# Self-attention stage of a fused two-layer block: where the row sums and the projections stand among the slots

## Chip, cores, metric

One core of one Trainium2 chip. The metric is the device time of one launch in microseconds; the median over runs counts. A profiled execution of the same kernel gives the trace.

## What is computed

The program is a stack of four blocks on x of 16 x 256 x 128 (batches, tokens, channels): an attention with a cross part, a gated feed-forward net, a pre-norm self-attention followed by a cross-attention (each with its own feed-forward net), and a routed expert layer. The change touches only the self-attention ("a1") of the third block. Cut to what matters, for each of the 16 batches and 16 heads of width 32:

```python
xn = _ln(x, lnx_g, lnx_b); yn = _ln(y, lny_g, lny_b)          # x is itself a LayerNorm of a LayerNorm
q = einsum('bsc,hcd->bhsd', xn, wq); k, v likewise from yn    # y is x here
a = softmax(einsum('bhsd,bhtd->bhst', q, k) * D ** -0.5)
mask = arange(t)[None, :] > arange(s)[:, None]                # causal: kept AFTER the softmax
o = einsum('bhst,bhtd->bhsd', a * mask, v)
x_out = x + o @ li1_w + li1_b
```

The softmax sums run over all 256 keys, the values only over the masked part, so sums and values are two different sets of products.

## The kernel before, in words

Every engine runs one program in the order in which it was written; semaphores tie the five programs together. The order inside this stage is written by hand in **slots**. `SelfAttention` has U = 8 slots to a batch; slot s belongs to unit s, a pair of heads. All four engines have a function for a slot (`tensor_slot` L1550, `vector_slot` L1621, `scalar_slot` L1686, `gpsimd_slot` L1731), and dictionaries (`SLOT` L1326, `VECTOR` L1327, `EARLY` L1328 for the last two batches) say at which slot, counted from 8n, each piece of batch n stands. Below, "slot 0" to "slot 7" is a slot's number modulo 8. `run` (L1757) emits slots 15 to 129; slots up to 14 are emitted between the products of the feed-forward stage before it (`l0_ffn`, L834, 16 slots to a step), the rest of the tail by `mha_ffn`. The parts of one slot:

- **Block** (`tensor_block`, L1474): 12 scores products and 12 products for the row maxima of a unit nine slots ahead, each on 32 rows of the array by 128 columns (L1499, L1504), then four products that subtract the maxima (L1511). The maxima go to PSUM banks 2 and 3, a single set: the next block waits until VectorE has reduced them (L1583). The scores go to banks 0 and 1, also a single set before batch 15: the next block waits for ScalarE's exp (L1668).
- **Sums** (`tensor_sums`, L1515) and **values** (`tensor_values`, L1532) of a group of four heads: products on 128 rows by 32 columns of the array. Sums of groups 0 to 3 stand at slots 2, 4, 6 and 8, values at 3, 5, 7 and 9, so that every slot has one of the two.
- **Projections** (`tensor_projection`, L1431), products on the whole array of 128 x 128: q0 at slot 0, k0 at 1, q1 at 2, k1 at 3, v0 at 4, v1 at 5, and at slot 6 z (two transposes), o (16 products, from slot 22 on) and nm (two transposes of the maxima). They share banks 5 and 7 through a ring of two. A q or k goes out through ScalarE (high half, L1652) and then VectorE (low half, L1593, one slot later); z goes out by four ScalarE activations (L1647). The third product of q0 (L1454) waits for `z_low`, which GpSimd writes (L1723) behind its select of slot 7 (L1705).
- **VectorE**, per slot: the maximum, then low halves of the projections of the slot before, then the pieces of `VECTOR` in its order: rden (L1611) and the first normalise (part 1, L187 on `b_zi`) in slot 6; scaled (L1619) in slot 0; stats of part 2 in slot 2; stats of part 0 (L150 to L159) in slot 4; second normalise (part 3, L187 on `b_z`) in slot 5; output in slot 7. Part 1 waits for GpSimd's reciprocal root (`gpsimd_rstd`, L161, of the kind "twice": six small operations, L172 to L181), which starts from the stats of part 0. Part 3 releases z.
- **ScalarE**, per slot: exp, the copy of the sums (L1684, slot 9), the copy of the values (L1676, slots 6 and 10), then the projections of the slot.

The piece of code that sets the order on TensorE:

```python
def tensor_slot(self, s):
    self.tensor_block(s)
    for g, n in self.parts(s, {0: 2, 1: 4, 2: 6, 3: 8}): self.tensor_sums(n, g)
    for g, n in self.parts(s, {0: 3, 1: 5, 2: 7, 3: 9}): self.tensor_values(n, g)
    for use in self.parts(s, self.SLOT): self.tensor_projection(use)
```

Of the kernel before, what the change touches and what calls it, by code (L numbers as in the profile page):

```python
# [241 lines left out]
def l0_attention(pr, mem, ffn, meanwhile):  # L242
# [56 lines left out]
    for i in range(3):  # L299
        nc.vector.memset(V[i][:, :, :, D:D + 1], 1.0)  # L300
        for a in range(2):
# [18 lines left out]

    SLOT = {"z": -28, "q0": -20, "q1": -16, "v": -14, "k": -15, "qk0": -24, "kc": -13, "ck": -23, "cv": -13,
            "qk1": -22, "nm": -3, "e0": 12, "e1": 13, "e2": 13, "e3": 18, "e4": 20}
# [3 lines left out]
    def batches(n, u, slots):  # L326

        pairs = [(part, *divmod(U * n + u - slot, U)) for part, slot in slots.items()]
        return [(part, batch) for part, batch, rest in pairs if rest == 0 and 0 <= batch < B]

    def projections(n, u):
        return batches(n, u, SLOT)

# [442 lines left out]
    for slot in (tensor_slot, vector_slot, scalar_slot, gpsimd_slot):  # L776
        for s in range(U * FIRST, tail):
            slot(s)
    sync_program()
    return Tail(tail, last, tensor_slot, vector_slot, scalar_slot, gpsimd_slot, exp_done, U * B, ys_ready, 3 * B,  # L780
                av_done, NV * B, x_done)

# [531 lines left out]
class SelfAttention:  # L1314
# [8 lines left out]

    U, G, D = 8, 4, 32

    SLOT = {"z": -18, "q0": -16, "k0": -15, "q1": -14, "k1": -13, "v0": -12, "v1": -11, "o": 22, "nm": -2}  # L1326
    VECTOR = {"rden": 14, "scaled": 16, "output": 23, 0: -28, 1: -26, 2: -22, 3: -19}  # L1327
    EARLY = {"o": 15, "rden": 9, "scaled": 12, "output": 16}  # L1328
    FIRST_MAX, FIRST, LAST = -9, -28, 8 * (B - 1) + 16
    tail_vector, tail = 8 * B + 1, 8 * B + 2  # L1330
# [3 lines left out]
    def __init__(self, pr, mem, tag, w):  # L1334
# [30 lines left out]
        for s in range(self.FIRST, self.LAST + 1):  # L1365
            for use in self.parts(s, self.SLOT):
                self.ring.add(use, "v" if use[0][0] in "qk" else "a")
# [181 lines left out]

    def tensor_slot(self, s):  # L1550
        self.tensor_block(s)
        for g, n in self.parts(s, {0: 2, 1: 4, 2: 6, 3: 8}):
            self.tensor_sums(n, g)
        for g, n in self.parts(s, {0: 3, 1: 5, 2: 7, 3: 9}):
            self.tensor_values(n, g)
        for use in self.parts(s, self.SLOT):
            self.tensor_projection(use)
# [63 lines left out]
    def vector_slot(self, s):  # L1621
        nx, m = divmod(s - self.FIRST_MAX, self.U)
        if 0 <= nx < B:
            self.vector_max(nx, m)
        for use in self.parts(s - 1, self.SLOT):
            if use[0][0] in "qk":
                self.vector_low(use)
        for part, n in self.parts(s, self.VECTOR):
            if part == "rden":
# [56 lines left out]
    def scalar_slot(self, s):  # L1686
# [5 lines left out]
        for half, n in self.parts(s, {0: 6, 1: 10}):  # L1692
            self.scalar_values(n, half)
        for use in self.parts(s, self.SLOT):
            self.scalar_projection(use)
# [76 lines left out]
class CrossAttention:  # L1772
# [10 lines left out]
    SLOT = {"z": -11, "k": -8, "q0": -7, "q1": -6, "v": -4, "nm": -1, "o": 14}  # L1783
    SCORES, VALUES, MAXIMA = {0: 0, 1: 2}, {0: 3, 1: 5}, -4
# [952 lines left out]
```

## Time and profile before

| | us |
|---|---|
| median of 3 runs | 1507.75 |
| the three runs | 1508.36, 1507.75, 1500.03 |
| profiled execution, its own time | 1501.43 |
| its span in the trace | 1499.7 |
| TensorE busy in the span | 1351.0 (90%) |
| VectorE / ScalarE / GpSimd busy | 977.7 / 845.7 / 649.5 |
| this stage alone (slot 15 to slot 129) | about 660 to 1015 in the span |

Mean granted clock of TensorE over the span: 0.967. A row of the timeline reads: start in us, duration in us, engine, line, operation, output <- inputs, shapes, count, and in brackets how long the engine was idle before it and what released it.

### The profile page before, as it was taken

Reading aid. Unit: us, or ns where it says so; the run is one execution under the profiler, and the core shown is the slowest. Engines: PE = TensorE matmul, PEld = TensorE weight load, DVE = VectorE, ACT = ScalarE, POOL = GpSimd, SP = SyncE. Lnnn points to the kernel's source line nnn. Section 1 sums busy time; section 2 is a strip of 40 time slices with the busy share of each in tenths; the row PEclk is TensorE's granted clock in tenths of the full one; section 3 lists DMA queues with packets and bytes.
Section 4 is the critical chain, followed back from the end, with each engine's and each line's share of the span. In section 5 each row is a group of like instructions: output and inputs, shape, how many; then the busy total and the mean of one; then the engine's idle time right before and its main releaser. Section 6 shows DMA issues by size and latency. Waiting matters only on the chain.

```text
span 1499.7 us, 42738 instructions
## 1 busy us (share of the span) xinstructions
PE 1351.0 (90%) x17848; PEld 856.9 (57%) x17848; DVE 977.7 (65%) x2238; ACT 845.7 (56%) x1309; POOL 649.5 (43%) x1118
## 2 busy tenths in 40 slices
PE   5899999997899998899999999997989999998695
PEld 2455555554344444455666666664766777677484
DVE  4777777775454544577788787745667887675232
ACT  2577777775465555657666666653456666432231
POOL 3355545543200001335666566343337775354155
PEclk9999999998999999999999999998999999998798
DMA  6000000000600000000000000012001111032351
GB/s 214 3 3 2 3 2 3 3 3 2 161 1 1 1 1 0 1 2 17 30 17 31 30 17 31 22 39 57 1 16 45 56 48 45 29 99 73 122 158 43
DMA packets 54514, 53.76 MB, mean 36 GB/s; under 512 B 9273, under 2 KB 48574, under 8 KB 54067
## 3 DMA queue, kind: packets, MB, share of 16 engines
q1 hardware_dynamic: 50482, 44.24, 9.7%
q0 software_dynamic: 2816, 6.11, 1.2%
q8 instruction: 142, 2.33, 0.7%
q10 hardware_dynamic: 1024, 0.69, 0.2%
q14 instruction: 50, 0.40, 0.1%
HBM read 20.34 MB, written 14.49 MB: 23 GB/s over the span
## 4 chain that ended last, share of the span: by engine, by line
PE 65%; DVE 12%; ACT 6%; issue 5%; POOL 5%; DMA 3%; SPq 3%; POOLq 0%; DVEq 0%; ACTq 0%
PE psum L1499 6%; PE psum L911 4%; PE psum L913 3%; PE psum L912 3%; PE psum L1182 3%; PE psum L1527 3%; DVE a_nm L580 3%; PE psum L1148 3%; PE psum L2496 2%; PE psum L2512 2%; PE psum L1976 2%; SPq L772 2%; DMA a_QT<-a_nmT 2%; DVE b_nm L1583 2%; PE psum L1985 2%
## 5 line engine op out<-in xcount | busy, mean ns | idle before, releaser
L1583 DVE TENSOR_REDUCE b_nm<-psum 128x4 f16<-128x1024 f32 x128 | 157.5, 1230 | 70.0 <-PE psum L1504 69.0
L697 ACT ACTIVATE a_prob<-psum 128x768 f32<-128x768 f32 (+1 forms) x160 | 136.1, 853 | 62.5 <-PE psum L460 60.6
L580 DVE TENSOR_REDUCE a_nm<-psum 128x4 f16<-128x1024 f32 (+1 forms) x96 | 117.4, 1223 | 50.2 <-PE psum L487 35.8
L749 POOL TENSOR_SCALAR_AFFINE_SELECT a_prob<-a_prob 128x512 f32<-128x512 f32 x128 | 81.7, 639 | 129.5 <-ACT a_prob L697 129.3
L170 POOL TENSOR_TENSOR f_ln_rstd<-f_ln_tmp,pow_half 128x4 f32<-128x4 f32 x24 | 25.3, 1056 | 204.6 <-DVE f_ln_tmp L159 204.6
L1040 ACT ACTIVATE xo_sb<-psum,f_w_h_s 128x512 f32<-128x512 f32 x64 | 44.0, 688 | 87.0 <-PE psum L913 87.0
L1499 PE MATMUL psum<-b_QTh,b_KTh 32*128 32x256 f16 x512 | 71.2, 272 | 11.7 <-DVE b_nm L1583 8.5
L1504 PE MATMUL psum<-b_KTh,b_QTh 32*128 32x256 f16 x512 | 70.7, 273 | 1.5 <-DVE b_nm L1583 1.5
L1499 PE MATMUL psum<-b_QTh,b_KTl 32*128 32x256 f16 x512 | 70.2, 268 | 0.0
L1499 PE MATMUL psum<-b_QTl,b_KTh 32*128 32x256 f16 x512 | 70.2, 267 | 0.0
L1504 PE MATMUL psum<-b_KTl,b_QTh 32*128 32x256 f16 x512 | 69.5, 268 | 0.0
L1504 PE MATMUL psum<-b_KTh,b_QTl 32*128 32x256 f16 x512 | 69.5, 268 | 0.0
L1705 POOL TENSOR_SCALAR_AFFINE_SELECT b_late<-f_hT1l 128x256 f32<-128x256 f32 x64 | 28.2, 463 | 88.7 <-ACT f_hT1l L1668 88.7
L2606 POOL DMA_INDIRECT out_dram<-m_ys,m_number x40 | 39.7, 991 | 55.2 <-DVE m_ys L2547 45.1
L980 DVE TENSOR_TENSOR f_hlastl<-xo_sb,f_hlasth 128x512 f16<-128x512 f32 x32 | 22.2, 692 | 53.0 <-ACT f_hlasth L1041 53.0
L980 DVE TENSOR_TENSOR f_hT1l<-xo_sb,f_hT1h 128x512 f16<-128x512 f32 x32 | 22.5, 702 | 51.6 <-ACT f_hT1h L1041 51.6
L911 PE MATMUL psum<-f_hT0h,f_h_wh 128*128 128x512 f16 x128 | 50.1, 392 | 5.9 <-DVE f_hT0l L974 5.9
L1499 PEld LDWEIGHTS psum<-b_QTh,b_KTh 32*128 32x128 f16 x512 | 25.4, 92 | 45.3 <-issue 27.8
L913 PE MATMUL psum<-f_hT0h,f_h_wl 128*128 128x512 f16 x128 | 50.0, 391 | 0.0
L912 PE MATMUL psum<-f_hT0l,f_h_wh 128*128 128x512 f16 x128 | 49.8, 389 | 0.0
L1511 PE MATMUL psum<-b_nmT,b_group_row 32*128 32x256 f16 x512 | 49.1, 268 | 0.0
L1668 ACT ACTIVATE f_hT0h<-psum 128x1024 f32<-128x1024 f32 x32 | 32.7, 1023 | 28.2 <-PE psum L1511 28.2
(448 smaller groups left out, 4637.8 us busy)
## 6 DMA issues: line engine op xcount, KB each, us to landing
f_h_wh<-b_rden SPq DMA_DIRECT2D x64, 128.0 KB, 2.1
f_h_wh<-c_rden SPq DMA_DIRECT2D x64, 128.0 KB, 2.1
expert_in<-empty SPq DMA_DIRECT2D x8, 662.5 KB, 11.0
m_xt<-expert_in SPq DMA_DIRECT2D x8, 662.5 KB
m_w<-in_L_ffn_w_dram SPq DMA_DIRECT2D x16, 256.0 KB
x_sb<-in_x_dram SPq DMA_DIRECT2D x8, 256.0 KB, 4.6
f_w_h_w<-in_L_ffn_h_w_dram SPq DMA_DIRECT2D x2, 1024.0 KB, 7.5
out_dram<-m_send SPq DMA_DIRECT2D x8, 256.0 KB, 2.5
```

The costliest lines, as they stand in the source:

```text
L580: nc.vector.tensor_reduce(out, psum[:, 2:4, :].rearrange("p i (a b) -> p i a b", a=groups), X, ALU.max, negate=True).then_inc(max_done, 1)
L697: nc.scalar.activation(prob[unit % 5][:, :, 0:width], psum[:, first:first + 2, 0:width], ACT.Exp, scale=SCALE).then_inc(exp_done, 1)
L749: nc.gpsimd.affine_select(out=diagonal, in_=diagonal, compare_op=ALU.is_ge, fill=0.0, base=0, pattern=[[0, 4], [1, P]], channel_multiplier ...
L911: nc.tensor.matmul(bank, wh[:, k, m * P:m * P + P], xh[:, k, :], start=(k == 0), stop=False)
L912: nc.tensor.matmul(bank, wh[:, k, m * P:m * P + P], xl[:, k, :], start=False, stop=False)
L913: inst = nc.tensor.matmul(bank, wl[:, k, m * P:m * P + P], xh[:, k, :], start=False, stop=(k == K4 - 1))
L1148: nc.tensor.matmul(psum[:, u % 3, :], li2[:, slot * P:slot * P + P], zT[n % 2][:, :], start=True, stop=True).then_inc(full, 1)
L1182: inst = nc.tensor.matmul(bank[:, to], hT[n % 2][:, k, to], li3[:, k, :], start=(t == 0 and k == 0), stop=True, skip_group_check=True)
L1499: t.matmul(psum[:, first_bank + i, to], key[r, g, own], q[r, g, :], start=(k + first + second == 0), stop=False, skip_group_check=True)
L1504: inst = t.matmul(psum[:, 2 + i, to], q[r, g, own], key[r, g, :], start=(k + first + second == 0), stop=(first == 1), skip_group_check=True)
L1511: inst = t.matmul(psum[:, first_bank + i, k * T:k * T + T], self.group_row[r, g, :], self.nmT[n % 2][r, :], start=False, stop=True, skip_g ...
L1583: v.tensor_reduce(self.nm[:, :, :].rearrange("p t (j r) -> p j t r", r=32)[:, 2 * e:2 * e + 2, :, g], self.pr.psum[:, 2:4, :].rearrange("p ...
```

## The change

Four edits, all of order; no instruction is added or removed.

1. `SLOT`: k0 moves from slot 1 to slot 0 (beside q0), k1 from 3 to 2 (beside q1), v1 from 5 to 4 (beside v0). Their exits on ScalarE, and the low halves on VectorE, move with them.
2. Sums move one slot later, to 3, 5, 7 and 9, right ahead of the values of the same group.
3. `VECTOR`: part 1 moves from -26 (slot 6, behind rden) to -27 (slot 5, ahead of part 3).
4. The slots of the values get a name.

```diff
-    SLOT = {"z": -18, "q0": -16, "k0": -15, "q1": -14, "k1": -13, "v0": -12, "v1": -11, "o": 22, "nm": -2}
-    VECTOR = {"rden": 14, "scaled": 16, "output": 23, 0: -28, 1: -26, 2: -22, 3: -19}
+    SLOT = {"z": -18, "q0": -16, "k0": -16, "q1": -14, "k1": -14, "v0": -12, "v1": -12, "o": 22, "nm": -2}
+    VALUES = {0: 3, 1: 5, 2: 7, 3: 9}
+    VECTOR = {"rden": 14, "scaled": 16, "output": 23, 0: -28, 1: -27, 2: -22, 3: -19}
...
     def tensor_slot(self, s):
         self.tensor_block(s)
-        for g, n in self.parts(s, {0: 2, 1: 4, 2: 6, 3: 8}):
+        for g, n in self.parts(s, self.VALUES):
             self.tensor_sums(n, g)
-        for g, n in self.parts(s, {0: 3, 1: 5, 2: 7, 3: 9}):
             self.tensor_values(n, g)
         for use in self.parts(s, self.SLOT):
             self.tensor_projection(use)
```

## Rows read from the trace of the kernel before

**Rows 1.** The page, first part: busy time of each engine.

```profile
PE 1351.0 (90%) x17848; PEld 856.9 (57%) x17848; DVE 977.7 (65%) x2238; ACT 845.7 (56%) x1309; POOL 649.5 (43%) x1118
```

**Rows 2.** Timeline of VectorE: maxima of slots 54, 55, 57, 58, 62, 110, one low half.

```profile
809.66 1.23 DVE L1583 TENSOR_REDUCE b_nm<-psum 128x4 f16<-128x1024 f32 x1 [0.79 <-PE psum L1504]
...
814.36 1.23 DVE L1583 TENSOR_REDUCE b_nm<-psum 128x4 f16<-128x1024 f32 x1 [1.39 <-PE psum L1504]
...
819.48 1.23 DVE L1583 TENSOR_REDUCE b_nm<-psum 128x4 f16<-128x1024 f32 x1 [0.41 <-PE psum L1504]
...
820.62 0.68 DVE L1593 TENSOR_TENSOR b_QTl<-psum,b_QTh 128x512 f16<-128x512 f32 x1
...
822.01 1.23 DVE L1583 TENSOR_REDUCE b_nm<-psum 128x4 f16<-128x1024 f32 x1 [0.71 <-PE psum L1504]
...
832.54 1.23 DVE L1583 TENSOR_REDUCE b_nm<-psum 128x4 f16<-128x1024 f32 x1 [0.79 <-PE psum L1504]
...
969.78 1.23 DVE L1583 TENSOR_REDUCE b_nm<-psum 128x4 f16<-128x1024 f32 x1 [1.29 <-PE psum L1504]
```

**Rows 3.** Timeline of TensorE, first instruction of the parts of slots 54 to 58.

```profile
809.75 0.41 PE L1527 MATMUL psum<-f_hT0h,b_group_col 128*32 128x256 f32 x2
...
810.75 0.44 PE L1439 MATMUL psum<-ident,b_z 128*128 128x128 f32 x2
...
813.25 0.28 PE L1464 MATMUL psum<-ident,b_nm 128*128 128x128 f16 x2 [0.27 <-ACT b_zTyh L1647]
813.47 0.28 PE L1499 MATMUL psum<-b_QTh,b_KTh 32*128 32x256 f16 x2
...
814.44 0.30 PE L1543 MATMUL psum<-f_hT0h,b_V 128*32 128x128 f32 x2
...
815.73 0.28 PE L1499 MATMUL psum<-b_QTh,b_KTh 32*128 32x256 f16 x2 [0.43 <-DVE b_nm L1583]
...
818.05 0.28 PE L1454 MATMUL psum<-b_zTxl,b_wqh 128*128 128x256 f16 x1
...
819.56 0.30 PE L1543 MATMUL psum<-f_hT1h,b_V 128*32 128x128 f32 x2
...
820.36 0.28 PE L1450 MATMUL psum<-b_zTyh,b_wkh 128*128 128x256 f16 x1
...
821.12 0.28 PE L1499 MATMUL psum<-b_QTh,b_KTh 32*128 32x256 f16 x2
```

**Rows 4.** Timeline of TensorE in the feed-forward stage: a block directly ahead of a whole-array product.

```profile
623.36 0.27 PE L1504 MATMUL psum<-b_KTl,b_QTh 32*128 32x256 f16 x2
623.47 0.27 PE L1504 MATMUL psum<-b_KTh,b_QTl 32*128 32x256 f16 x2
623.67 0.39 PE L911 MATMUL psum<-f_hT0h,f_h_wh 128*128 128x512 f16 x1
```

**Rows 5.** Timeline of GpSimd: select of slot 55, low of z, first and last step of a reciprocal root.

```profile
815.65 1.07 POOL L1705 TENSOR_SCALAR_AFFINE_SELECT b_late<-f_hT1l 128x256 f32<-128x256 f32 x2 [3.92 <-ACT f_hT1l L1668]
...
817.33 0.66 POOL L1723 TENSOR_TENSOR b_zTyl<-b_zTy,b_zTyh 128x256 f16<-128x256 f32 x1
...
830.07 0.69 POOL L172 TENSOR_TENSOR b_lni_tmp<-b_lni_tmp,pow_one 128x2 f32<-128x2 f32 x1 [0.72 <-DVE b_lni_tmp L159]
...
832.98 0.20 POOL L181 TENSOR_TENSOR b_lni_rstd<-b_lni_rstd,b_lni_tmp 128x2 f32<-128x2 f32 x1
```

**Rows 6.** Timeline of ScalarE in slot 54: the first activation of z.

```profile
811.26 0.57 ACT L1647 ACTIVATE b_zTx<-psum,b_w_bx,b_w_gx 128x256 f32<-128x256 f32 x1
```

**Rows 7.** Timeline of VectorE in the feed-forward stage, around part 1 of batches 1 and 2.

```profile
602.34 0.60 DVE L187 TENSOR_SCALAR b_z<-u_sb,b_lnx_mv,b_lnx_rstd 128x128 f32<-128x128 f32 x2
...
618.30 0.75 DVE L969 SCALAR_TENSOR_TENSOR xo_sb<-psum,f_w_w_s,xo_sb 128x512 f32<-128x512 f32 x1 [0.60 <-PE psum L904]
...
620.90 0.60 DVE L187 TENSOR_SCALAR b_zi<-x_sb,b_lni_mv,b_lni_rstd 128x128 f32<-128x128 f32 x2 [1.25 <-POOL b_lni_rstd L181]
```

**Rows 8.** Timeline of GpSimd there: last step of the reciprocal root of batch 1.

```profile
603.66 0.19 POOL L181 TENSOR_TENSOR b_lni_rstd<-b_lni_rstd,b_lni_tmp 128x2 f32<-128x2 f32 x1
```

## The prediction

> **What bounds the kernel now.** I read the page's busy shares first, then the timelines of TensorE, VectorE, GpSimd and ScalarE over one batch of the stage. TensorE is busy 90% of the span [rows 1], but that is no proof that each slot is bound by it, so I went slot by slot. The maximum of slot 54 starts at 809.66, that of slot 62 at 832.54, that of slot 110 at 969.78 [rows 2]: 22.88 for one batch, and (969.78 - 809.66) / 7 = 22.87 for the seven up to there. The pattern repeats exactly from the batch in which o first stands (slot 22) to slot 110, eleven times. Within it:
> - Slot 6 lasts 814.36 - 809.66 = 4.70 [rows 2]. The nm transposes waited 0.27 for the last activation of z on ScalarE [rows 3], so the end of slot 6 is ScalarE's: exp, copy of the values, four activations of z. TensorE's own work there is hidden.
> - Slot 7 lasts 815.73 - 813.47 = 2.26; the next block waited 0.43 for the maximum [rows 3]. This is VectorE's floor for any slot: its maximum begins 814.36 - 813.47 = 0.89 behind the block and the next block 1.37 behind that [rows 2, 3].
> - Slots 0 to 5 are TensorE's. Slots 7 and 0 together are 819.48 - 814.36 = 5.12, slot 1 is 822.01 - 819.48 = 2.53, slots 2 to 5 are 832.54 - 822.01 = 10.53 [rows 2].
>
> **What a turn of the array costs.** In a block successive steps stand 0.11 apart, but from its last step to a whole-array product it is 623.67 - 623.47 = 0.20 [rows 4]: 0.09 for the change of shape. A k projection is six steps of 0.107, 0.64, yet the next block comes 821.12 - 820.36 = 0.76 after its start [rows 3]: 0.12. So a turn is about 0.09 to 0.13. Parts with the turn behind them: block 814.44 - 813.47 = 0.97, sums 810.75 - 809.75 = 1.00, values 820.36 - 819.56 = 0.80, q or k (v likewise, three products of twice the columns) 0.76 [rows 3]. Sums and values use the array in the same shape, so between them I take no turn: sums 0.87. Bounds: 0 and 0.13 for it.
>
> [...]
>
> **The change, one batch.**
> - Slots 2 to 5. Even ones become block + two projections, 0.97 + 0.64 + 0.76 = 2.37; odd ones block + sums + values, 0.97 + 0.87 + 0.80 = 2.64. Four slots are 10.02 instead of 10.53: -0.5. With a turn of 0.13 between sums and values it is -0.25; I take -0.45. Even slots stay above the floor of 2.26 by 0.11, and VectorE's two low halves now follow each other: the low begins 820.62 - 819.48 = 1.14 after the maximum and takes 0.68, of which some 0.6 is its own time [rows 2], so both end 2.4 after the maximum, before the next one, due after 2.64.
> - Slot 1: 2.64 to 2.67 instead of 2.53: +0.13. It loses k0 and gets the last sums.
> - Slots 7 and 0. The sums of group 2 leave slot 6, where they were hidden, for slot 7, whose 2.26 was VectorE's: it becomes about 2.66. Slot 0 then cannot use that delay: q0's third product needs the low half of z. GpSimd starts the select of slot 7 at 815.65 and ends the second low at 817.33 + 0.66 = 817.99 [rows 5], and the product went at 818.05, 4.58 behind block 7's start [rows 3]. That chain (exp of slot 7, select, two lows) hangs on block 7 and not on what TensorE does after it, so it stays 4.58. TensorE would now be there at 2.66 + 0.97 + 0.22 = 3.85, and waits 0.73. Behind it come four q0 steps, 0.43, and k0 with its turn, 0.76: 4.58 + 1.19 = 5.77 instead of 5.12: +0.65. What queues behind the waiting product: k0, block 1, and so the next maximum; nothing else fills TensorE.
> - Slot 6. Taking the sums out gives nothing, since ScalarE's chain sets its end. And part 1 is now in slot 5, in VectorE's queue ahead of part 3 and of the maximum of slot 6. Its root takes GpSimd 832.98 + 0.20 - 830.07 = 3.11 [rows 5] and was ready at 833.18, 0.64 after the maximum of slot 6 began [rows 2]. The stats start 0.60 earlier (k1's low no longer stands ahead of them), but slots 4 and 5 are 0.21 shorter, so the root comes 0.64 - 0.60 + 0.21 = 0.25 after the moment when that maximum is due. Then a hop of about 0.1, part 1 and part 3 (two normalise operations each, 0.60 a part in rows 7, some 0.45 when another follows at once): the maximum starts 1.4 late and z is released only then. Before, z went to TensorE 810.75 - 809.66 = 1.09 and to ScalarE 811.26 - 809.66 = 1.60 after the maximum [rows 2, 3, 6]; now TensorE gets it at about 1.44 and ScalarE at 1.95. So z, which was followed by everything else on ScalarE, is 0.35 later: +0.35. The late maximum itself is covered by slot 6's length, and so is rden behind it, barely (it ends about when block 7 starts; the next maximum is 0.89 later). Bounds: 0, if the root comes in time, and +1.4, if nothing covers it.
>
> Batch: -0.45 + 0.13 + 0.65 + 0.35 = +0.68. Eleven of them: +7.5.
>
> **The rest of the stage.** The two batches of slots 6 to 21 have no o; there exp of slot 7 waits behind z and the same two waits bite: +0.7 each, 1.4. At the end no projections are left: slots 110 and 118 lose the sums' 1.00 each; slots 111, 113, 115, 117 and 119 go from 2.26 to 2.66, +2.0; slots 120 to 127 lose a turn or two per pair, four times 0.25. Together -1.0.
>
> In the feed-forward stage ahead, slots are long, but VectorE's queue also holds that stage's own work. Part 1 of batch 2 waited 1.25 there, at 620.90 [rows 7]. One slot earlier it stands ahead of part 3 and of the gated product of 618.30 [rows 7], which would then start at 620.9 + 0.45 + 0.60 = 621.95, 3.65 late; z's four activations stand in ScalarE's queue ahead of the next GELU, so TensorE's next layer is up to 3.6 late too. For batch 1 the root ended at 603.66 + 0.19 [rows 8] while part 3 ran at 602.34 [rows 7]: z would be released 2.1 late, of which TensorE had about 0.9 idle to spare: 1.2. The two are 4.8 at most; some is absorbed where TensorE later waited for VectorE anyway. I take +4.0, bounds 0 and +6.
>
> Other edits: the order in the ring of banks is the same (q0, k0, q1, ...), so each part gets the bank that it had; the exits on ScalarE move with their slot and stay ahead of the next exp; the SyncE queue is untouched, rden and its four transfers keep their slots; naming the slots is nothing.
>
> **Sum.** +7.5 + 1.4 - 1.0 + 4.0 = +11.9. On the profiled execution's own 1501.43 that is 1513.3. Two of the three runs shown stand some 7 above it; on the median, 1507.75, it is 1519.7, and I give 1519.5.
>
> **Rivals.**
> - *Only the junctions and slot 7 matter.* Part 1 costs nothing (GpSimd's root is in time, or the feed-forward stage swallows it). Then a batch is +0.34 (0.65 + 0.13 - 0.45), thirteen of them 4.4, less 1.0: 1507.75 + 3.4 = 1511. For it: much of what part 1 delays is idle time; against it: 0.25 late by the rows, in strict order. 15%.
> - *Faster: both waits on GpSimd are hidden.* The place is q0's third product. If the low half of z landed by 3.85 behind block 7 instead of 4.58 (a shorter select and shorter lows, if the 1.07 of rows 5 was a collision with VectorE), slots 7 and 0 would be 5.04, -0.08, and with part 1 free the batch 0.13 - 0.45 - 0.08 = -0.40. Thirteen: -5.2, less 1.0: 1507.75 - 6.2 = 1501.5. It decides from 0.4 us gained on that chain. Against it: the exp and the select alone take 815.65 + 1.07 - 813.47 = 3.25 [rows 3, 5], and nothing in the change shortens them. 10%.
> - *The stall spreads.* Part 1's wait pushes the maximum, rden, its transfers and the late selects, and slot 6 grows by 1.0 to 1.4 rather than 0.35: +0.7 to +1.0 a batch more, 9 to 13 in all: 1530. For it: rden is covered by nothing to spare. 20%.
>
> **How the numbers follow.** Forecast 55%, the others 15, 10 and 20. About 1%, 15 us, is what a measurement of this kernel can tell from no change. The forecast's own range is 1512 to 1526, of which its top, 12 points, lies over +1%; the spreading stall lies over it nearly whole: slower 0.31. Of the fast rival 3 points are beyond -1%; the rest is within. The range for eight in ten reaches down to the fast rival's middle and up to the start of the spreading stall: 1503 to 1528.
>
> **What would show it.** In the profile after: no gap longer than 0.03 between sums and values, even slots of 2.37 and odd ones of 2.65 between maxima; in slot 0 a wait of some 0.7 at L1454 for GpSimd's low; part 1 on VectorE idle some 1.8 for the root (2.64 from maximum to maximum, less 1.14, plus 0.35), and the maximum of slot 6 late by 1.4; slots 6 of 5.05; a batch of 23.55. Wrong it would be if a batch came under 22.9, if L1454 didn't wait, or if the block of slot 7 waited for a maximum.

## The result, and the profile after

| | us |
|---|---|
| changed kernel, median of 4 runs | 1525.43 (1522.93 to 1529.46) |
| kernel before, 4 runs beside them | 1506.87 (1500.03 to 1508.36) |
| ratio, 95% interval | 1.0134 (1.0107 to 1.0162) |
| profiled execution after: own time, span | 1524.46, 1522.7 |
| profiled execution before: span | 1499.7 |

The kernel became 1.3% slower, 18.6 us by the medians and 23.0 by the two spans. The forecast was 1519.5, within 1503 to 1528. Most of its signs and places were right, the end of the stage was not, and the sum (+11.9) was too small. The mean granted clock is 0.954 (0.967 before).

The page's first part, of the kernel after, against [rows 1]: busy times hardly moved, the span grew. What came is waiting.

```profile
PE 1346.2 (88%) x17848; PEld 870.0 (57%) x17848; DVE 979.8 (64%) x2238; ACT 841.3 (55%) x1309; POOL 648.6 (43%) x1118
```

VectorE's timeline after, slots 52 to 57 (slots 4, 5, 6, 7, 0 and 1 of a batch), against [rows 2]:

```profile
811.55 1.23 DVE L1584 TENSOR_REDUCE b_nm<-psum 128x4 f16<-128x1024 f32 x1 [0.21 <-PE psum L1506]
...
813.93 1.23 DVE L1584 TENSOR_REDUCE b_nm<-psum 128x4 f16<-128x1024 f32 x1 [0.27 <-PE psum L1506]
816.85 0.69 DVE L187 TENSOR_SCALAR b_zi<-x_sb,b_lni_mv,b_lni_rstd 128x128 f32<-128x128 f32 x2 [1.69 <-POOL b_lni_rstd L181]
817.46 0.59 DVE L187 TENSOR_SCALAR b_z<-u_sb,b_lnx_mv,b_lnx_rstd 128x128 f32<-128x128 f32 x2
817.97 1.22 DVE L1584 TENSOR_REDUCE b_nm<-psum 128x4 f16<-128x1024 f32 x1
...
821.73 1.23 DVE L1584 TENSOR_REDUCE b_nm<-psum 128x4 f16<-128x1024 f32 x1 [0.89 <-PE psum L1506]
...
824.37 1.23 DVE L1584 TENSOR_REDUCE b_nm<-psum 128x4 f16<-128x1024 f32 x1 [0.54 <-PE psum L1506]
...
827.50 1.23 DVE L1584 TENSOR_REDUCE b_nm<-psum 128x4 f16<-128x1024 f32 x1 [0.37 <-PE psum L1506]
```

The third line is the first new wait: part 1 idles 1.69 for the root (forecast 1.8), part 3 and the maximum stand behind it, and that maximum starts at 817.97 where 813.93 + 2.64 = 816.57 was due: 1.40 late, as forecast. The next three rows give slots 6, 7 and 0 from maximum to maximum: 3.76, 2.64, 3.13.

TensorE's timeline after, slots 54 to 57, against [rows 3]:

```profile
818.19 0.41 PE L1441 MATMUL psum<-ident,b_z 128*128 128x128 f32 x2 [1.47 <-DVE b_z L187]
...
820.63 0.28 PE L1466 MATMUL psum<-ident,b_nm 128*128 128x128 f16 x2 [0.24 <-ACT b_zTyh L1648]
820.85 0.28 PE L1501 MATMUL psum<-b_QTh,b_KTh 32*128 32x256 f16 x2
...
821.82 0.41 PE L1529 MATMUL psum<-f_hT0h,b_group_col 128*32 128x256 f32 x2
...
822.28 0.39 PE L1529 MATMUL psum<-f_hT0h,b_group_col 128*32 128x256 f32 x2
...
822.50 0.39 PE L1529 MATMUL psum<-f_hT0h,b_group_col 128*32 128x256 f32 x2
...
822.71 0.28 PE L1545 MATMUL psum<-f_hT0h,b_V 128*32 128x128 f32 x2
...
823.48 0.28 PE L1501 MATMUL psum<-b_QTh,b_KTh 32*128 32x256 f16 x2
...
825.41 0.28 PE L1456 MATMUL psum<-b_zTxl,b_wqh 128*128 128x256 f16 x1 [0.56 <-POOL b_zTyl L1724]
...
826.61 0.28 PE L1501 MATMUL psum<-b_QTh,b_KTh 32*128 32x256 f16 x2
```

Three readings. From the last sums step to the values it is 822.71 - 822.50 = 0.21, the pace within the sums themselves (822.50 - 822.28 = 0.22): between two parts of one shape there is no turn. The product of L1456 waits 0.56 for the low half of z, the second new wait; it goes 825.41 - 820.85 = 4.56 behind block 7 (forecast 4.58, before 4.58), and block 1 goes 5.76 behind it (forecast 5.77). The idle of 1.47 ahead of z is not all loss: ScalarE's chain sets the end of slot 6, and before the change the sums filled part of that time.

GpSimd's timeline after, the chain of that low half, against [rows 5]: the select is released by the exp of slot 7 and again takes 1.07, both lows follow.

```profile
823.03 1.07 POOL L1706 TENSOR_SCALAR_AFFINE_SELECT b_late<-f_hT1l 128x256 f32<-128x256 f32 x2 [4.36 <-ACT f_hT1l L1669]
...
824.70 0.67 POOL L1724 TENSOR_TENSOR b_zTyl<-b_zTy,b_zTyh 128x256 f16<-128x256 f32 x1
```

The waits of TensorE after, from 690 to 940 us (engine, line, waited for: us in total, times, longest), show both in every batch:

```profile
PE psum L1441 <- DVE b_z L187: 16.2, 11, 1.5
PE psum L1456 <- POOL b_zTyl L1724: 5.1, 9, 0.6
PE psum L1466 <- ACT b_zTyh L1648: 2.4, 10, 0.2
```

Before, the same view had none of the first two:

```profile
PE psum L1499 <- DVE b_nm L1583: 4.3, 10, 0.4
PE psum L1464 <- ACT b_zTyh L1647: 2.7, 10, 0.3
```

VectorE's timeline after, in the last steps of the feed-forward stage ahead, against [rows 7]. Part 1 of batch 1 waits 1.54, that of batch 2 3.19 (before: none and 1.25), and here part 3 and the gated product are behind it.

```profile
599.16 0.60 DVE L187 TENSOR_SCALAR b_zi<-x_sb,b_lni_mv,b_lni_rstd 128x128 f32<-128x128 f32 x2 [1.54 <-POOL b_lni_rstd L181]
...
617.24 0.60 DVE L187 TENSOR_SCALAR b_zi<-x_sb,b_lni_mv,b_lni_rstd 128x128 f32<-128x128 f32 x2 [3.19 <-POOL b_lni_rstd L181]
617.76 0.60 DVE L187 TENSOR_SCALAR b_z<-u_sb,b_lnx_mv,b_lnx_rstd 128x128 f32<-128x128 f32 x2
618.27 0.75 DVE L969 SCALAR_TENSOR_TENSOR xo_sb<-psum,f_w_w_s,xo_sb 128x512 f32<-128x512 f32 x1
```

The end of the stage after, VectorE's timeline: here something came that no step had foreseen. The scaled products of batches 12 and 13 (batches are counted from 0) wait 1.93 and 5.41 for the broadcast of rden. The first and third rows are the maxima of slots 110 and 111.

```profile
981.35 1.23 DVE L1584 TENSOR_REDUCE b_nm<-psum 128x4 f16<-128x1024 f32 x1 [1.40 <-PE psum L1506]
982.49 1.74 DVE L1612 RECIPROCAL b_rden<-b_sums 128x256 f32<-128x256 f32 x1
984.42 1.23 DVE L1584 TENSOR_REDUCE b_nm<-psum 128x4 f16<-128x1024 f32 x1 [0.19 <-PE psum L1506]
...
990.22 1.23 DVE L1620 TENSOR_TENSOR f_h_wl<-f_h_wh 128x1024 f32<-128x1024 f32 x1 [1.93 <-DMA f_h_wh<-b_rden]
...
1004.55 1.74 DVE L1612 RECIPROCAL b_rden<-b_sums 128x256 f32<-128x256 f32 x1
...
1012.44 1.22 DVE L1620 TENSOR_TENSOR f_h_wl<-f_h_wl,f_h_wh 128x1024 f32<-128x1024 f32 x1 [5.41 <-DMA f_h_wh<-b_rden]
```

TensorE's next sums wait for the rden of batch 14, which stands behind the second of these waits in VectorE's queue:

```profile
1015.48 0.41 PE L1529 MATMUL psum<-f_hT0h,b_group_col 128*32 128x256 f32 x2 [2.65 <-DVE b_rden L1612]
```

Before, batch 12 had no wait on VectorE, and batch 13 had 2.44:

```profile
990.83 1.74 DVE L1611 RECIPROCAL b_rden<-b_sums 128x256 f32<-128x256 f32 x1
...
996.61 1.23 DVE L1619 TENSOR_TENSOR f_h_wl<-f_h_wl,f_h_wh 128x1024 f32<-128x1024 f32 x1 [2.44 <-DMA f_h_wh<-b_rden]
```

Where the 23.0 us of the two spans went, by stretches between the same instructions. The first stretch ends at the last GELU ahead of the last step of the feed-forward stage (603.02 before, 598.22 after); the next ones end at the maxima of slots 7, 23, 95 and 111, and at the first product of the next feed-forward stage. The forecast's -1.0 for slots 110 to 127 is split here by place: the 1.00 of slot 110 belongs to the stretch up to slot 111, which leaves 0.0 for the rest.

| stretch | before | after | difference | forecast |
|---|---|---|---|---|
| up to the last feed-forward step | 603.0 | 598.2 | -4.8 | 0 |
| from there to slot 7 | 74.6 | 82.1 | +7.5 | +4.0 |
| slots 7 to 23 (two batches, no o) | 45.2 | 47.0 | +1.8 | +1.4 |
| slots 23 to 95 (nine batches) | 205.9 | 212.5 | +6.6 | +6.1 |
| slots 95 to 111 (two batches) | 45.1 | 44.7 | -0.5 | +0.4 |
| slot 111 to the next stage | 47.0 | 53.3 | +6.3 | 0.0 |
| the rest of the program | 478.9 | 485.0 | +6.1 | 0 |

A full batch takes 212.47 / 9 = 23.61. Its eight slots after, from maximum to maximum, slot 6 first: 3.77, 2.63, 3.13, 2.63, 2.40, 2.63, 2.38, 4.03 (sum 23.60); before: 4.69, 2.26, 2.86, 2.53, 2.74, 2.53, 2.73, 2.53 (22.87). Slot 5's 4.03 holds the late maximum: without its 1.40 it is 2.63, and slot 6 is 5.17.

### The profile page after: what moved, and what is told of

It is laid out like the page before. It is cut to its first block, busy times and chain, and to the rows that moved or that the text cites. A ratio compares the mean times of both kernels' runs of the same rounds, so it can differ in the third digit from the quotient of the medians.

```text
span 1522.7 us, 42738 instructions
## 1 busy us (share of the span) xinstructions
PE 1346.2 (88%) x17848; PEld 870.0 (57%) x17848; DVE 979.8 (64%) x2238; ACT 841.3 (55%) x1309; POOL 648.6 (43%) x1118
## 4 chain that ended last, share of the span: by engine, by line
PE 55%; DVE 14%; POOL 10%; issue 8%; ACT 5%; DMA 4%; SPq 3%; POOLq 0%; DVEq 0%; ACTq 0%
PE psum L1501 4%; PE psum L1182 3%; PE psum L911 3%; PE psum L913 3%; PE psum L912 3%; DVE a_nm L580 3%; PE psum L1148 3%; PE psum L1529 2%; PE psum L2497 2%; PE psum L2513 2%; SPq L772 2%; POOL b_late L1706 2%; DMA a_QT<-a_nmT 2%; PE psum L1977 2%; DVE b_nm L1584 2%
## 5 line engine op out<-in xcount | busy, mean ns | idle before, releaser
L1669 ACT ACTIVATE f_hT1h<-psum 128x1024 f32<-128x1024 f32 x32 | 32.8, 1024 | 48.4 <-PE psum L1513 48.4
L911 PE MATMUL psum<-f_hT0h,f_h_wh 128*128 128x512 f16 x128 | 49.4, 386 | 6.6 <-DVE f_hT0l L974 6.6
```

The costliest lines, as they stand in the source:

```text
L911: nc.tensor.matmul(bank, wh[:, k, m * P:m * P + P], xh[:, k, :], start=(k == 0), stop=False)
L1669: a.activation(self.prob[unit % 4][:, :, :], self.pr.psum[:, first:first + 2, :], ACT.Exp, scale=self.SCALE).then_inc(self.exp_done, 1)
```

## The experiments

In all of them "batch" is the mean of slots 23 to 95 of the profiled execution, and "end" the stretch from slot 111 to the next feed-forward stage. A ratio is to the kernel before on the same chip. Kernels that ran only once have no interval; they are read by their stretches, which are steadier than whole times.

**The changed kernel again**, unedited, to see what is steady between executions.

> The changed kernel once more, to see which of its 18.6 us (1525.4 against 1506.9) come back in the same places. Theory A (waits by their place in strict queues): a steady batch of slots 22 to 94 lasts 23.60 again, the stall of VectorE for the four transfers of rden at slot 112 and the TensorE idle at slot 123 come again, ratio to before 1.013. Theory B (the part of the loss that lies behind the stage, some 6 us, is only the clock's history of one execution): batches as in A, but that part is gone or has another size.

Measured: 1523.73 (4 runs), ratio 1.0122 (1.0081 to 1.0164). Batch 23.60; up to slot 7 81.3 where the first profile had 82.1; end 50.6 where it had 53.3. The waits of VectorE at slot 112 (1.77) and of TensorE for the rden of batch 14 (1.81) came again, and the rest of the program took 485.4, as in the first profile: theory B is not borne out. So the batch repeats within 0.01, the end to 2.6 us.

**Part 1 back to its slot.**

```diff
-    VECTOR = {..., 0: -28, 1: -27, 2: -22, 3: -19}
+    VECTOR = {..., 0: -28, 1: -26, 2: -22, 3: -19}
```

> The changed kernel with part 1 of VectorE back in slot 6 behind rden. Theory A: slot 6 loses 0.35 and the maximum of slot 6 is on time, batch 23.25; the last step of the feed-forward stage ahead comes 3 to 4.5 us earlier; 8 to 10 us below the changed kernel, ratio to before about 1.007. Theory C (the two waits hide one another: with z earlier, q0 just waits longer for the low half of z): batch still over 23.5, and under 5 us in all.

Measured: 1510.08 (10 runs), ratio 1.0039 (1.0014 to 1.0064): 13.7 us less than the changed kernel beside it, where 8 to 10 had been expected. Up to slot 7 it takes 74.1, as before the change, 7.2 less than again; batch 23.14, 0.46 less; slots 7 to 23 1.0 less. The waits of TensorE, 690 to 940:

```profile
PE psum L1466 <- ACT b_zTyh L1648: 12.8, 10, 1.3
PE psum L1456 <- POOL b_zTyl L1724: 6.4, 11, 0.7
```

The wait for z is gone, and most of that idle time has moved to the nm transposes (1.3 for ScalarE): TensorE is no fuller in slot 6, the slot ends earlier all the same. So part 1's place is the largest single cost of the change, and of what it cost beyond the forecast (13.7 against 8.6) two thirds lie ahead of slot 7 (7.2 against 4.0).

**The low half of z one slot earlier on GpSimd**, ahead of the select of slot 7.

```diff
-        for part, n in self.parts(s, {"low": -17, ...}):
+        for part, n in self.parts(s, {"low": -18, ...}):
```

> The changed kernel with the low half of z on GpSimd one slot earlier (slot 6, ahead of the select of slot 7 instead of behind it); part 1 stays in slot 5. Theory A: the third product of q0 waits for nothing, slots 7 and 0 lose 0.7, batch 22.9, 9 to 10 us below the changed kernel, ratio to before about 1.006. Theory C: the late z of slot 6 is what counts, GpSimd's select of slot 7 now comes late instead and holds the values of slot 1 or the exp, batch over 23.4.

Measured: 1515.70 (7 runs), ratio 1.0082 (1.0048 to 1.0115), 8.0 us less than again (9 to 10 expected). Batch 22.96: four of the nine take 22.87, which is 0.73 less than again, and five take 23.01 to 23.08. In the same stretch VectorE waited five times, 1.9 us in all, for the transfers of rden. Slots 7 to 23 gain nothing. The waits of TensorE, 690 to 940: the line of L1456 is gone and nothing took its place.

```profile
PE psum L1441 <- DVE b_z L187: 16.1, 11, 1.5
```

**Both edits together.** Does one wait hide the other, or do they add?

> Both: part 1 back in slot 6 and the low half of z in slot 6 on GpSimd. Theory A: the two add up, batch 22.6, about 0.3 below the kernel before; the feed-forward stage as before; the tail still costs some 5 us, so ratio to before 0.997 to 1.002. Theory C: not below 23.2. If the grouping of sums and values cost TensorE time by itself, the odd slots would stay above 2.64.

Measured: 1502.28 (10 runs), ratio 0.9974 (0.9951 to 0.9997). Less than again by 21.5, against 13.7 + 8.0 = 21.7 for the two alone: they add, and the idea that one hides behind the other falls. Batch 22.47, which is -0.40 to before; five of the nine take 22.39, -0.48. This is the regrouping alone (the fast rival had -0.40 for it). Nine batches are 3.6 shorter than before, but the end is 50.1, 3.1 longer, and takes most of that back; with the smaller gains of the other stretches the stage as a whole is 4.4 shorter.

**Where should the sums of group 2 stand?** In both, with them left in slot 6, where they are hidden:

```diff
-        for g, n in self.parts(s, self.VALUES):
+        for g, n in self.parts(s, {0: 3, 1: 5, 2: 6, 3: 9}):
             self.tensor_sums(n, g)
+        for g, n in self.parts(s, self.VALUES):
             self.tensor_values(n, g)
```

> Both moves of the run before, and the sums of group 2 stay in slot 6, where the kernel before had them (groups 0, 1 and 3 stand with their values in slots 3, 5 and 9). Theory A: slot 6 is ScalarE's, so the sums cost nothing there, slot 7 goes back to VectorE's floor of 2.26, and the distance from rden to scaled grows by nothing less than before: batch 22.0, some 0.9 below the kernel before; ratio 0.989 to 0.992. Theory D (the sums in slot 6 were not hidden; the gain of 'both' needs the pairs everywhere): batch not below 22.4.

Measured: 1496.50 (10 runs), ratio 0.9935 (0.9913 to 0.9957), so 0.65% faster than the kernel before (0.989 to 0.992 had been expected). Batch 22.03, end 46.6. VectorE's timeline of it, slots 7, 0 and 1:

```profile
831.86 1.23 DVE L1585 TENSOR_REDUCE b_nm<-psum 128x4 f16<-128x1024 f32 x1 [1.39 <-PE psum L1506]
...
834.12 1.23 DVE L1585 TENSOR_REDUCE b_nm<-psum 128x4 f16<-128x1024 f32 x1 [0.16 <-PE psum L1506]
...
836.73 1.22 DVE L1585 TENSOR_REDUCE b_nm<-psum 128x4 f16<-128x1024 f32 x1
```

Slot 7 is at VectorE's floor again, 834.12 - 831.86 = 2.26, and slot 0 is 2.61: with the low half early, the 0.37 saved in slot 7 are no longer waited away in slot 0.

**The same move of the sums in the changed kernel itself**, both waits left in.

> The changed kernel with the sums of group 2 back in slot 6 and nothing else. Theory A: slot 7 falls from 2.63 to 2.26, but the low half of z hangs on block 7 and q0's third product waits that much longer, so slots 7 and 0 stay 5.77 together and a batch 23.60. Theory G (the move of the sums out of slot 6 is what costs): batch 23.2.

Measured (one run): 1526.21. Batch 23.60, unchanged to the hundredth: slot 7 shrinks to 2.26 and slot 0 grows to 3.50. So the product that waits for the low half is tied to block 7, as the forecast had it, and not to what TensorE does in between. But the end is 47.0, as long as before the change (again: 50.6): the longer end comes with the sums of group 2 in slot 7. All fourteen profiles of this document agree: six have these sums in slot 7 and rden at its old slot, with ends of 49.4 to 53.3; the other eight have ends of 46.6 to 47.4.

**One half of the regrouping at a time, in the kernel before.** First the sums alone, with their values:

```diff
-        for g, n in self.parts(s, {0: 2, 1: 4, 2: 6, 3: 8}): self.tensor_sums(n, g)
+        for g, n in self.parts(s, {0: 3, 1: 5, 2: 7, 3: 9}): self.tensor_sums(n, g)
```

> The kernel before with the sums alone moved beside the values; the projections stay one to a slot. Theory A: odd slots become block, sums, values, projection, 0.97 + 0.87 + 0.80 + 0.76 = 3.4, while even slots cannot go under VectorE's floor of 2.26: batch 24.3 to 24.6, 20 us or more above the kernel before, although TensorE has fewer turns. Theory E (turns are what counts): batch below 22.9.

Measured (one run): 1531.07, batch 24.51, +1.64. Its waits of TensorE, 700 to 960:

```profile
PE psum L1464 <- ACT b_zTyh L1647: 12.7, 10, 1.3
PE psum L1499 <- DVE b_nm L1583: 9.7, 21, 0.5
PE psum L1454 <- POOL b_zTyl L1723: 6.3, 11, 0.7
```

Then the projections alone, two to an even slot:

```diff
-    SLOT = {"z": -18, "q0": -16, "k0": -15, "q1": -14, "k1": -13, "v0": -12, "v1": -11, ...}
+    SLOT = {"z": -18, "q0": -16, "k0": -16, "q1": -14, "k1": -14, "v0": -12, "v1": -12, ...}
```

> The kernel before with the projections alone paired in even slots. Theory A: even slots 0.97 + 1.00 + 0.64 + 0.76 = 3.4, odd ones at the floor of 2.26: batch 23.6 to 23.9, some 12 us above the kernel before. Theory E: about as before, 22.9.

Measured (one run): 1518.44, batch 24.04, +1.16. Its waits of TensorE, 700 to 960:

```profile
PE psum L1499 <- DVE b_nm L1583: 17.9, 42, 0.4
```

Each half alone takes turns of the array away and is slower. A slot that loses a part falls only to what VectorE needs, while its neighbour pays the part in full. With the projections alone, the odd slots take 2.26 to 2.34 and TensorE waits there (17.9 us in 42 blocks, about four in each batch), and the even ones 3.31 to 3.52. With the sums alone, slots 2 and 4 take 2.61 and not 2.26: VectorE works through them without a pause, on the maximum, a low half and the stats of a part, so the floor of these slots is higher than that of slot 7. Only the two halves together leave the slots even, 2.38 and 2.63. The batch with the sums alone lies in the expected range, the one with the projections alone above it (24.04 where 23.6 to 23.9 was expected).

**Part 1 one slot earlier, in the kernel before.**

```diff
-    VECTOR = {..., 0: -28, 1: -26, 2: -22, 3: -19}
+    VECTOR = {..., 0: -28, 1: -27, 2: -22, 3: -19}
```

> The kernel before with part 1 of VectorE alone in slot 5. Theory A: z late by VectorE's wait for the root: 7 to 8 us lost before slot 7 of the first batch as in the changed kernel, and 0.4 to 0.7 a batch, batch 23.3 to 23.6; 12 to 16 us above the kernel before. Theory C (the wait costs only where slots 4 and 5 are already shortened): batch 22.9.

Measured (one run): 1533.06, batch 24.27, +1.40, far more than in the changed kernel. Its waits of VectorE, 700 to 960:

```profile
DVE b_zi L187 <- POOL b_lni_rstd L181: 21.3, 11, 1.9
DVE f_h_wl L1619 <- DMA f_h_wh<-b_rden: 7.5, 7, 1.9
```

The expectation missed. In the kernel before, the low half of k1 stands ahead of the stats of part 0, so the root is later: part 1 starts 0.64 after the moment when the maximum of slot 6 was due, and 0.28 after it in the changed kernel. z goes to TensorE 2.28 after that moment, and slot 6, counted from it, takes 5.82 where it took 4.69 (in the changed kernel 1.62 and 5.17). Six of the nine batches take 24.01, +1.14, which is this and nothing else. The other three take 24.15 to 25.45 and make up the remaining 0.26 of the mean; that they are longer by VectorE's waits for rden's transfers fits the view above, but was not tried. The regrouping, then, made part 1's new place cheaper, not dearer. Ahead of slot 7 the damage is about the same as in the changed kernel (82.4 against 74.6).

**The low half early, in the kernel before.**

> The kernel before with the low half of z alone moved ahead of the select of slot 7 on GpSimd. Theory A: with q0 behind the sums it hardly waited, so only the 0.1 of slot 0 goes: batch 22.75 to 22.87. Theory H (GpSimd's order was a cost of its own in the kernel before): batch under 22.5.

Measured (one run): 1505.19 beside 1505.99; batch 22.77, 0.1 less. Before the change there was nothing there to win: the edit matters only once TensorE arrives early.

**Rden one slot earlier**, at slot 13 and behind part 3, first in the kernel with both edits:

```diff
-    VECTOR = {"rden": 14, "scaled": 16, "output": 23, 0: -28, 1: -26, 2: -22, 3: -19}
+    VECTOR = {"scaled": 16, "output": 23, 0: -28, 1: -26, 2: -22, 3: -19, "rden": 13}
```

> The run 'both' with rden one slot earlier, in slot 5 behind part 3 instead of slot 6, so that its four transfers have 1.6 us more before scaled asks for them. Theory A (the end of the stage loses its time because the shorter slots leave the transfers of rden no room: VectorE waits for them at slot 112, and at slots 118 to 123 this holds rden of batch 14, so TensorE idles for some 3 us and its granted clock falls): those waits go, from slot 111 to the next stage 47 us instead of 50.1, granted clock 1.00 there, batches 22.40 throughout instead of 22.39 to 22.70. Theory F (the end is slow for the longer odd slots alone): 111 to the next stage stays near 50.

Measured: 1496.93 (4 runs), ratio 0.9939 (0.9919 to 0.9958). Batch 22.40, end 46.6, that is 3.5 less than in both. At the end of the stage VectorE has no wait for batch 12 and 0.80 for batch 13, where both has 2.06 and 5.28. (The edit moves the rden of batches 0 to 13; the last two keep theirs, by `EARLY`.)

```profile
986.84 1.23 DVE L1620 TENSOR_TENSOR f_h_wl<-f_h_wl,f_h_wh 128x1024 f32<-128x1024 f32 x1 [0.80 <-DMA f_h_wh<-b_rden]
```

**The same in the kernel called best above.**

> The run 'best' with rden one slot earlier as well. Theory A: a batch stays 22.03, since slots 7 to 1 are bound by VectorE's maxima, scaled and low halves there, and the few late transfers go: from slot 111 to the next stage 46 or less, 1 to 2 us below 'best' at most; ratio 0.990 to 0.994. If rden in slot 5 made the maximum of slot 6 late enough to hold nm, the batch would be above 22.3.

Measured: 1497.58 (8 runs), ratio 0.9944 (0.9924 to 0.9964), batch 22.03, end 47.0. Nothing more is won, against an expected end of 46 or less: the two cures for the end don't add, as each already removes the same late transfers. The three fastest kernels can't be told apart; each beats both the kernel before and the changed one.

## Why the prediction was right, and where it was not

**Right by its own steps.** Slots 2 to 5: forecast -0.45, measured 2.40 + 2.63 + 2.38 + 2.63 = 10.04 against 10.53, -0.49. Slot 1: +0.13, measured +0.10. Slots 7 and 0: +0.65, measured 2.63 + 3.13 = 5.76 against 5.12, +0.64, by the mechanism named (the wait itself was 0.56 and not 0.73, since TensorE got there at 4.00 and not 3.85, but the product goes by the low half of z, at 4.56); with the low half early it vanished, and after_g2 showed that it hangs on block 7. No turn between sums and values; even slots 2.38 to 2.40 (forecast 2.37), odd ones 2.63 (2.65). The batch: 23.60 against 23.55. Nine batches and the two without o cost 8.4 (forecast 7.5). The Trainium skill (TensorE: Matmul & The Clock Gate, Single matmul latency) puts the time for results to drain from the array at roughly 175 ns; as an estimate from that page, taking it as the price of each of four turns saved, slots 2 to 5 would have won 4 x 0.175 = 0.70. The measurement is -0.49, nearer to the 0.09 to 0.13 a turn that the rows of the kernel before gave.

**Slot 6, the term mis-sized.** "+0.35" was +0.48. The root came 0.17 after the moment when the maximum was due (it ended at 816.54 + 0.20 = 816.74 on GpSimd, against 816.57), a little sooner than my 0.25, but the two normalise parts took 0.61 and 0.59 where I had taken "some 0.45 when another follows at once". So z went to TensorE 818.19 - 816.57 = 1.62 after that moment instead of 1.44.

**The feed-forward stage ahead, the term mis-sized.** "I take +4.0" was +7.5 up to slot 7 in the first profile and +6.7 in the second; with part 1 back it was -0.5. I had added up two waits at the places where they stand (1.2 and 3.6, in full 4.8) and let some be absorbed. Nothing was absorbed: by the two profiles, 1.7 and 1.4 were lost ahead of the last step, where z of batch 1 was late (for the 1.2), and 4.3 in both within that step, from its first SiLU to its last sum on VectorE (for the 3.6). Another 1.5 and 1.0 came between the step and slot 7, for which I had no term. Part 1 altogether: forecast 0.35 x 13 + 4.0 = 8.6, measured 13.7 by the medians. That is where most of the gap between +11.9 and the +18.6 of the medians lies.

**The end of the stage, the step that failed.** "At the end no projections are left: ... Together -1.0." There I had counted TensorE's parts only. Those came out: slot 110 took 4.07 before (969.78 to 973.85) and 984.42 - 981.35 = 3.07 after, and in both_rden, where no transfer is late, the stretch from slot 111 is -0.3 where the parts gave 0.0. The transfers of rden I had put at nothing, with the words "rden and its four transfers keep their slots". That is true of the slots and was no argument: the time from issue to landing changed. From slot 111 it was +6.3, in the second profile +3.7. The fourth transfer of batch 12 landed 4.07 after its issue where it had taken 2.12, which is the whole of VectorE's new wait of 1.93; that of batch 13 took 4.23 instead of 2.13, which is 2.1 of the growth from 2.44 to 5.41. With the sums of group 2 out of slot 7, or with rden a slot earlier, the end is 46.6 to 47.0, as before the change (47.0). That these edits remove the extra 3.1 to 3.7 is shown; why the transfers land late stands in the last section, as does TensorE's clock, by which the first profile's end is longer still.

**Slots 95 to 111.** They took 0.5 less where +0.4 was forecast. The two new waits cost what they cost elsewhere, but the last part 1 (batch 15) stands in slot 93, so slot 102 was not lengthened, and the pattern that I extended to slot 110 ends there.

**How much was luck.** The measured 1525.4 lies inside 1503 to 1528, and only just inside the forecast's own range of 1512 to 1526. The top of the wider range stood where it did for a spreading stall, which did not come; the end of the stage, which did, had no term at all.

**The rivals.** "Only the junctions and slot 7 matter" falls: part 1 cost more than anything else. "Faster: both waits on GpSimd are hidden" did not happen, but its price was right: with both waits taken away the batch is -0.40 in the mean, -0.48 in five of the nine (forecast -0.40), and the medians 1502.28 against 1505.03. "The stall spreads" falls in this form: slot 6 grew by 0.48, not by 1.0 to 1.4. In the kernel before, part 1 alone does reach that size (slot 6 +1.13, the batch +1.40), though mostly by z itself and only for 0.26 by rden's transfers. What did spread by way of rden and its transfers is the end of the stage.

**Open.** The rest of the program, where not a line changed its work, took 478.9 us in the one profile of the kernel before and 479.5 to 486.0 in the thirteen others. Before's profiled execution was itself 5.4 below the median of its runs (1501.43 against 1506.87), so this part says more on that execution than on the change, and the difference of the medians (18.6) is the better measure of the change. The first stretch, too, lies anywhere from 598.2 to 608.5 in the profiles, in no order that the edits explain.

## What to carry to other kernels

In a slot schedule written by hand, an instruction that waits should be placed by the time at which its input is ready, not by the slot in which it is needed: put ahead of its time it holds back all that stands behind it in its engine's queue, and here over half of its cost arose where that queue also served another stage. Before regrouping work to save turns of the array, find each slot's floor on the other engines (here 2.26 to 2.61 on VectorE, by what else stands in the slot), since a lighter slot only wins down to that floor and its neighbour pays in full. When TensorE is made to arrive earlier at a product, look at once at what that product reads: the gain of 0.4 to 0.5 us a batch was there, but only after the producer on GpSimd had been moved one slot as well.

## What the hardware showed that I had not expected

**Broadcasts that land late by the share of one DMA engine.** Rden's broadcast is four transfers of 128 KB. In the kernel before (batch 13) all four land within 2.0 to 2.1 us of their issue; in the changed kernel three do, and the fourth takes 4.2, although the issues stand at the same distance from rden. The DMA view of the changed kernel for 1009.2 to 1010.4 (rate over 40 slices, then the queues that had packets):

```profile
GB/s 137 103 35 0 0 0 0 0 205 205 205 410 273 307 410 273 375 307 341 273 206 137 137 34 0 0 0 0 0 0 0 0 0 546 0 0 0 0 0 0
...
q8 instruction: 1, 0.02, 4.8%
```

and for 1010.4 to 1012.4:

```profile
GB/s 0 0 0 0 0 0 0 0 0 0 0 0 0 0 20 0 20 0 20 0 0 20 0 20 0 20 0 20 0 20 0 0 0 0 0 0 0 0 0 0
DMA packets 9, 0.01 MB, mean 4 GB/s; under 512 B 1, under 2 KB 9, under 8 KB 9
```

At 1010.2 one packet of the instruction queue (0.02 MB) passes; its 4.8% of 16 engines over 1.2 us are 0.92 us of one engine. Behind it, from 1011.1, nine packets of the broadcast (eight of data and one of under 512 B) come one by one, 0.1 us apart; 1010.2 and 0.92 make 1011.1, so they begin as the instruction packet ends. The four transfers are 576 packets, 144 each, and 144 / 16 = 9: one of the 16 DMA engines moved its share of the last transfer after all the others had finished, and VectorE waited for it. In the kernel before, the instruction packet passes at 996.0 to 996.3, when the broadcast is nearly through, and the landing stays at 2.1. With rden a slot earlier (both_rden) no instruction packet falls between issue and landing of batch 13's broadcast, and it lands in 2.1. Over all fourteen profiles, the distance from rden to scaled of batch 13 is one of two kinds: 5.8 to 5.9 where the sums of group 2 stand in slot 6 (and in both_rden), and 7.0 to 7.9 where they stand in slot 7. So a shift of the program by a part decides whether a fetch of code meets a transfer.

It is not special to the end of the stage. The fourteen profiles hold 224 of these broadcasts. In 64 of them no instruction packet fell between the first issue and the last landing, and in every one of the 64 the fourth transfer landed in 2.1. In 83 it took 2.8 or more, up to 4.3, and every one of the 83 had such a packet; in 82 of them it began between 0.3 ahead of the fourth issue and 1.6 behind it (in the one shown above 2.0 behind). In the remaining 77 broadcasts a packet fell at another moment, and the landing stayed under 2.4. The kernel before had late landings too, in batches 2, 4, 6 and 8 (3.2 to 3.6), and its batches were 22.87 all the same. That the fetch is the cause fits all of these, but no run moved the fetch alone, and the delay of 2.1 is more than the 0.92 that its packet took: the cause is argued, not shown.

**The clock.** The windows of the changed kernel at the end of the stage (us, busy times of PE, PEld, DVE, ACT and POOL, granted clock, DMA share, GB/s):

```profile
1012.00:1018.00 6.00, 3.35 (x70) 2.30 (x60) 2.89 (x2) 2.43 (x3) 1.64 (x5) 0.89 0.16 53
1018.00:1024.00 6.00, 6.00 (x82) 3.67 (x80) 0.00 (x0) 1.94 (x2) 1.53 (x4) 0.54 0.11 37
```

After a stretch in which TensorE was busy 3.35 of 6.00 us, it worked for 6 us at 0.54 of full speed, mostly at the lower level of 1.2 GHz; from 1003 to 1012 the clock had been 1.00. In both, nearly the same wait (2.52, here 2.65) left the clock at 1.00:

```profile
997.00:1003.00 6.00, 3.48 (x86) 2.62 (x78) 2.89 (x2) 2.60 (x4) 1.53 (x4) 1.00 0.20 66
1003.00:1012.00 9.00, 9.00 (x148) 7.04 (x143) 1.99 (x3) 4.68 (x6) 3.75 (x9) 1.00 0.05 18
```

In the second profile of the changed kernel (again) the clock was 0.72 from 1019 to 1025 and 1.00 from 1025 to 1031, behind a wait of 1.81. What the lower clock cost can be estimated from these means: 6.00 x 0.11 + 6.00 x 0.46 = 3.4 us of full speed in the first profile, 6.00 x 0.28 = 1.7 in again, nothing in both. The ends, 53.3, 50.6 and 50.1, differ by about as much: of the 2.6 between the two profiles of one kernel, 1.7 is the clock and 0.8 the shorter wait. So a wait at the end of a stage can cost more than its own length, but need not, and of this end's 6.3 us some 3.4 are, by this estimate, the clock. Why it fell in one execution and not in the other is open.
